# Masked attention on one core: a second, transposed score matmul in place of normalised and turned probabilities

## The reference, cut to what matters

```python
src_trans = (einsum('bsf,of->bso', src, W_src) + b_src) * src_mask[:, :, None]
tgt_trans = (einsum('btf,of->bto', tgt, W_tgt) + b_tgt) * tgt_mask[:, :, None]
src_key, src_val = jnp.split(src_trans, 2, axis=2)
scores = einsum('bthd,bshd->bhts', q, k) / np.sqrt(HEAD_DIM)
scores = where(src_mask[:, None, None, :] == 0, -inf, scores)
attn = softmax(scores, axis=-1)
tgt_update = einsum('bhts,bshd->bthd', attn, v).reshape(b, t, OUT_SIZE)
x = x + tanh(g) * (concatenate([tgt, tgt_update], axis=2) @ W_out.T + b_out)
```

## Time and profile before

| what | us |
| --- | --- |
| median of 3 runs | 712.64 (712.11 to 713.82) |
| the profiled execution | 712.77 |
| its span, first to last instruction | 710.7 |
| scores of batch 0 start | 276.31 |
| scores of batch 15 start | 594.39 |

### The profile page before, as it was taken

One profiled execution on the slowest core, in us unless ns is written; L12 is line 12 of the kernel. 1 busy time (PEld: TensorE's weight loads), 2 busy tenths in 40 slices (PEclk: granted clock), 3 DMA queues, 4 the chain that ended last, 5 costly groups with the idle time before them and its releaser, 6 DMA issues.

```text
span 710.7 us, 12199 instructions
## 1 busy us (share of the span) xinstructions
PE 681.4 (96%) x3877; PEld 478.4 (67%) x3877; DVE 512.4 (72%) x976; ACT 418.1 (59%) x1128; POOL 209.7 (30%) x285
## 2 busy tenths in 40 slices
PE   5799899999999999999999999999999998999997
PEld 3565555554544358788888888888888886756654
DVE  7864757776775458898889888888888888734422
ACT  7656665535555535656756657657667657645453
POOL 6564424200110033233343432332323330052110
PEclk9999999999999999999999999999999999999999
DMA  8721108401000004444323444333444323001012
GB/s 260 237 101 60 59 31 253 79 6 56 1 0 1 0 1 119 120 120 119 76 79 88 119 120 100 87 76 94 119 119 92 85 47 74 3 0 60 30 60 89
DMA packets 44970, 57.54 MB, mean 81 GB/s; under 512 B 13018, under 2 KB 23420, under 8 KB 44796
## 3 DMA queue, kind: packets, MB, share of 16 engines
q1 hardware_dynamic: 44924, 56.96, 29.8%
HBM read 27.46 MB, written 4.19 MB: 45 GB/s over the span
## 4 chain that ended last, share of the span: by engine, by line
PE 79%; ACT 7%; DVE 6%; issue 3%; POOL 2%; SPq 1%; DMA 1%; DVEq 0%; ACTq 0%; POOLq 0%
PE bank L1160 11%; PE bank L1456 8%; PE bank L1374 7%; PE bank L1435 7%; PE bank L1172 5%; PE bank L1392 5%; ACT c_p L956 5%; PE bank L1413 4%; PE bank L1449 4%; PE bank L1592 4%; PE bank L1136 3%; PE bank L1582 2%; PE bank L1140 2%; PE bank L1583 2%; DVE c_nmx L1914 2%
## 5 line engine op out<-in xcount | busy, mean ns | idle before, releaser
L956 ACT ACTIVATE c_p<-bank,c_nmx 128x256 f32<-128x256 f32 x256 | 117.3, 487 | 26.2 <-DVE c_nmx L1914 26.2
L1160 PE MATMUL bank<-b_o,cw 128*128 128x512 f32 x192 | 90.8, 603 | 0.2 <-ACT b_o L808 0.2
L1927 DVE TENSOR_TENSOR c_p<-c_p,c_inv 128x1024 f32<-128x1024 f32 x64 | 90.1, 1408 | 1.1
L1914 DVE TENSOR_REDUCE c_nmx<-bank 128x4 f32<-128x1024 f32 x64 | 75.4, 1218 | 13.4 <-PE bank L1413 13.4
L1435 PE MATMUL bank<-ident,c_p 128*128 128x128 f32 x512 | 65.4, 276 | 2.2 <-ACT c_p L956 1.6
L1435 PEld LDWEIGHTS bank<-ident,c_p 128*128 128x128 f32 x512 | 58.2, 142 | 10.0 <-issue 4.5
L784 ACT ACTIVATE b_h<-bank,cb 128x512 f32<-128x512 f32 x48 | 32.8, 686 | 51.2 <-PE bank L1160 51.2
L1059 ACT ACTIVATE d_h<-bank,b_col 128x512 f32<-128x512 f32 x64 | 39.6, 686 | 39.6 <-PE bank L1583 39.6
L1374 PE MATMUL bank<-c_ctxT,wsrcT 128*128 128x256 f32 x256 | 61.4, 385 | 0.7 <-ACT c_ctxT L932 0.7
L1160 PEld LDWEIGHTS bank<-b_o,cw 128*128 128x128 f32 x192 | 34.1, 190 | 41.3 <-issue 39.2
L1934 DVE COPY c_pT<-bank 128x512 f32<-128x512 f32 x64 | 43.7, 685 | 18.0 <-PE bank L1435 18.0
(11 more groups left out here) (194 smaller groups left out, 1384.4 us busy)
## 6 DMA issues: line engine op xcount, KB each, us to landing
c_stack<-c_parts SPq DMA_DIRECT2D x192, 128.0 KB
a_ctx<-in_ctx SPq DMA_DIRECT2D x16, 512.0 KB, 3.8
c_ctx<-in_ctx SPq DMA_DIRECT2D x16, 512.0 KB, 3.5
out_x<-x_sb SPq DMA_DIRECT2D x7, 512.0 KB, 2.9
x_sb<-in_x SPq DMA_DIRECT2D x3, 1024.0 KB, 10.2
mask_b<-in_mask_BxS_fk SPq DMA_DIRECT2D x1, 2048.0 KB, 12.1
x_sb<-in_x SPq DMA_DIRECT2D x2, 512.0 KB, 5.9
wsrc_raw<-in_L_xattn_W_src SPq DMA_DIRECT2D x1, 1024.0 KB, 6.8
```

Source lines behind the costliest of these rows:

```text
L956: op = nc.scalar.activation(c_p[hg][:, tc, j, :], scores(tc)[:, j, :], ACT.Exp, bias=c_nmx[hg][:, tc, j:j + 1], accum_out=c_sum[hg][:, tc, ...
L1160: op = mm(bank[2 * u + h][:], cw1[:, c, h * P:(h + 1) * P], b_o[n % LANES][:, c, :], start=c == 0, stop=c == DK - 1)
L1914: v.tensor_reduce(c_nmx[hg][:, tc, :], scores(tc), AXIS.X, ALU.max, negate=True)\
L1927: v.tensor_tensor(pr, pr, c_inv[hg][:, :, js].unsqueeze(3).to_broadcast([P, TS, 2, S]), ALU.mult)\
```

## The change: what it does

The probabilities are no longer kept, normalised and turned. The exps of the scores are taken only for their sums, into a bf16 buffer that nobody reads (`c_junk`). From maximum and sum each token and head gets the shift -max - ln(sum), with a correction from 1/sum x sum. It is split into two fp32r parts, turned by PE (4 heads x 2 parts = 8 columns, one transpose per tile), copied by ACT into `c_rows` and moved by a DMA into rows 97 and 98 of the query side of the stack; the key side has ones there. Then the scores are computed a second time with keys as the stationary side, over 99 rows, which gives the transposed and shifted scores in the same banks 0 to 3, and one exp per tile of 1024 elements writes `c_pT` directly. The functions Exp, Ln and Copy are taken from one table set, which is asked for once before the stage.

The weights of keys and queries are loaded with the order of heads and head elements exchanged, so that a stack DMA takes all 128 partitions of a part: 6 DMAs instead of 12, keys and queries apart. `ones_c` fills rows 96 to 98 of both sides. In the last batch, two hidden matmul groups of the next stage are put ahead of the last update. Waits on the old semaphores are replaced by waits on `c_sum_ok`, `c_pT_ok` and others; `scores_free`, `turned_bank` and `ASIDE` are gone. Cut to its core:

```diff
 # SP
-            def stack_c(b, s): ... 12 DMAs, then neg_row
+            def sides_c(b, s, side, firsts):
+                for c, part in enumerate(firsts):
+                    sp.dma_start(c_stack[s][c * HD:(c + 1) * HD, side, ...], c_parts[:, part, ...]).then_inc(c_stack_in, 16)
+            def keys_c(b, s):
+                need(sp, c_k_split, 2 * b + 2)
+                need(sp, c_sT_ps, 2 * TS * (b - 1))
+                sides_c(b, s, 1, (K_HI, K_HI, K_LO))
+            def queries_c(b, s):
+                need(sp, c_qlo_ok, b + 1)
+                sides_c(b, s, 0, (Q_HI, Q_LO, Q_HI))
+                ... neg_row DMA
+            def rows_c(b, s, hg):
+                sp.wait_ge(c_rows_ok, 2 * b + hg + 1)
+                sp.dma_start(c_stack[s][MASK_ROW + 1:MASK_ROW + 1 + SHIFTS, 0, :, hg, :], c_rows[hg][:]).then_inc(c_rows_in, 16)
+            for b in range(B):   # after keys, queries of 0 and stream 2
+                rows_c(b - 1, ., 1); keys_c(b + 1, .); rows_c(b, ., 0); queries_c(b + 1, .); stream_c(b + 3, .)
+            rows_c(B - 1, 1, 1)
 # ACT
-            def exps_c(b, hg, tc):        # into c_p
-            def probsT_c(b, hg, heads):   # copies bank -> c_pT
+            def sums_c(b, hg, tc):
+                need(act, c_mx_ok, TS * n + tc + 1)
+                need(act, c_shift_ok, n - 1)
+                for j in range(QH):
+                    op = nc.scalar.activation(c_junk[:, tc, j, :], scores(tc)[:, j, :], ACT.Exp,
+                                              bias=c_nmx[hg][:, tc, j:j + 1], accum_out=c_sum[hg][:, tc, j:j + 1])
+                op.then_inc(c_sum_ok, 1)
+            def logs_c(b, hg):
+                need(act, c_sum_ok, TS * (n + 1))
+                nc.scalar.activation(c_ln[hg][:], c_sum[hg][:], ACT.Ln).then_inc(c_ln_ok, 1)
+                need(act, c_ln_ok, n + 1)
+                nc.scalar.activation(c_inv[hg][:], c_ln[hg][:], ACT.Exp, scale=-1.0).then_inc(c_inv_ok, 1)
+            def rows_c(b, hg):
+                need(act, c_rows_ps, n + 1)
+                nc.scalar.copy(c_rows[hg][:], bank[6][0:SHIFTS * QH, hg * S:(hg + 1) * S]).then_inc(c_rows_ok, 1)
+            def probsT_c(b, hg, q):
+                need(act, c_sT_ps, TS * n + q + 1)
+                nc.scalar.activation(c_pT[hg][:, :, q * S:(q + 1) * S], scores(q), ACT.Exp).then_inc(c_pT_ok, 1)
 # order on ACT in body_c
+                rows(b-1,1), sums(b,0,0), sums(b,0,1), logs(b,0), probsT(b-1,1,0), high_q, probsT(b-1,1,1),
+                ctxT, update(b-1,1), v, ctxT, rows(b,0), sums(b,1,0), sums(b,1,1), logs(b,1),
+                probsT(b,0,0), probsT(b,0,1), xnT, xnTq, update(b,0)
+            nc.scalar.preload_act_table_set("natural_log_exp_and_others")
 # PE
+            def rows_c(b, hg):
+                need(pe, c_shift_ok, n + 1)
+                need(pe, c_up_ok, n - 1 if is_last(b, B) and hg == 1 else n)
+                for tc in range(TS):
+                    op = nc.tensor.transpose(bank[6][0:SHIFTS * QH, hg * S + tc * P:hg * S + (tc + 1) * P],
+                                             c_shift[hg][:, tc, :, :] as [128, 8], ident[:])
+                op.then_inc(c_rows_ps, 1)
+            def scoresT_c(b, s, hg, q):
+                need(pe, c_rows_in, 16 * (n + 1))
+                need(pe, c_sum_ok, TS * (n + 1) + q + 1)      # the last half: c_pT_ok
+                for j in range(QH):
+                    op = mm(scores(q)[:, j, :], c_stack[s][rows, 1, j, hg, q * P:(q + 1) * P],
+                            c_stack[s][rows, 0, j, hg, :], start=True, stop=True)
+                op.then_inc(c_sT_ps, 1)
 # order on PE in body_c
+                scores(b,0), rows(b-1,1), q, v0, scoresT(b-1,1,0), ctxT, scoresT(b-1,1,1), out_begin(b-1), v1,
+                update(b-1,1), scores(b,1), ctxT, rows(b,0), out(b-1), k first half, scoresT(b,0,0), scoresT(b,0,1),
+                k second half, xnT, update(b,0)
 # order on PE in last_c and after it
+                scores(b,0), rows(b-1,1), lowrank_d(0), xnT_d(1,1), out_begin(b-1), scoresT(b-1,1,0), scoresT(b-1,1,1),
+                scores(b,1), update(b-1,1), xnT_d(1,0), rows(b,0), out(b-1), scoresT(b,0,0), lowrank_d(1),
+                scoresT(b,0,1), rows(b,1), update(b,0)
+            out_begin(b), scoresT(b,1,0), scoresT(b,1,1), hidden_d(0,0), hidden_d(0,1), update(b,1), out(b)
 # DVE
-            inverse_c, normalise_c, probsT_c
+            def shift_c(b, hg):   # five operations on [128, TS, QH], each waits for the one before
+                c_fix = c_inv * c_sum;  c_fix = c_fix - 1 + c_ln;  c_fix = c_nmx - c_fix
+                c_shift hi = c_fix (to fp32r);  c_shift lo = c_fix - hi
+            # in body_c: shift(b,0) before v(b+1) and maxima(b,1); shift(b,1) after finish(b-1)
 # POOL
-                nc.gpsimd.memset(c_stack[s][MASK_ROW:MASK_ROW + 1, 0, :, :, :], 1.0)
+                nc.gpsimd.memset(c_stack[s][MASK_ROW:MASK_ROW + 1 + SHIFTS, :, :, :, :], 1.0)
```

More of the change, by code:

```diff
@@ L64 @@
 MASK_ROW = 3 * HD
-STACK_DMAS = 3 * QH + 1
+STACK_DMAS = 7
+SHIFTS = 2
 LEAD = 2
@@ L516, in stream_c @@
                 sp.dma_start(c_ctx[s][:], ctx_dram[b]).then_inc(c_ctx_in[s], 16)
-            def stack_c(b, s):
-                if isinstance(b, int) and b == 1:
-                    sp.wait_ge(b_ok[3], 2 * PAIRS)
[L521 to L529, removed]
+            def sides_c(b, s, side, firsts):
+                for c, part in enumerate(firsts):
+                    sp.dma_start(
+                        c_stack[s][c * HD:(c + 1) * HD, side, :, :, :].rearrange("p j g t -> p j (g t)").bitcast(F32),
+                        c_parts[:, part, :, :].rearrange("p g t -> p (g t)").bitcast(F32)).then_inc(c_stack_in, 16)
+            def keys_c(b, s):
+                if b == 1:
+                    sp.wait_ge(b_ok[3], 2 * PAIRS)
+                need(sp, c_k_split, 2 * b + 2)
[4 more added lines that the diff above has]
+                sides_c(b, s, 0, (Q_HI, Q_LO, Q_HI))
+                if b < 2:
+                    sp.wait_ge(s_ones, b + 1)
                 sp.dma_start(
@@ L1004, in body_c @@
                     return
-                exps_c(b, 0, 0)
-                exps_c(b, 0, 1)
                 if not first:
-                    probsT_c(b - 1, 1)
-                if not last:
-                    high_q(b + 1)
+                    rows_c(b - 1, 1)
+                sums_c(b, 0, 0)
+                sums_c(b, 0, 1)
+                logs_c(b, 0)
+                if not first:
+                    probsT_c(b - 1, 1, 0)
+                high_q(b + 1)
+                if not first:
+                    probsT_c(b - 1, 1, 1)
                 if ahead:
@@ L1415, in scores_c @@
                     op.then_inc(c_s_ps, 1)
-            def probsT_c(b, hg, heads=range(QH)):
+            def rows_c(b, hg):
                 n = 2 * b + hg
[L1419 to L1431, removed]
-                            pe.wait_ge((c_pT_act, c_pT_dve)[j % 2], QH // 2 * n + 1)
-                    for q in range(TS):
-                        for tc in range(TS):
-                            op = nc.tensor.transpose(
-                                bank[turned_bank(n, j)][:, q * S + tc * P:q * S + (tc + 1) * P],
-                                c_p[hg][:, tc, j, q * P:(q + 1) * P], ident[:])
-                    op.then_inc(c_pT_ps, 1)
@@ L1516, in body_c @@
                 scores_c(b, s, 0)
-                if not last:
-                    q_c(b + 1, 1 - s)
-                    v_c(b + 1, 1 - s, 0)
+                if not first:
+                    rows_c(b - 1, 1)
+                q_c(b + 1, 1 - s)
+                v_c(b + 1, 1 - s, 0)
                 if first:
@@ L1526, in body_c @@
                 if not first:
-                    probsT_c(b - 1, 1, range(2, QH))
-                if not first:
+                    scoresT_c(b - 1, 1 - s, 1, 1)
                     out_begin(b - 1, 1 - s)
-                if not last:
-                    v_c(b + 1, 1 - s, 1)
+                v_c(b + 1, 1 - s, 1)
                 if not first:
```

253 lines of the change are left out of this document (133 added, 120 removed).

## The result

The changed kernel takes **738.25 us** (median of 4 runs, 734.92 to 742.33) against 712.61 (712.11 to 713.82): a ratio of 1.036, 95% interval 1.0306 to 1.0414. It is slower by 25.6 us. The forecast was 703.8 with a range of 698.5 to 712, and 0.15 for slower. The profiled execution took 737.84 us (span 735.4, mean clock 0.985; before 712.77 and 710.7).

A forecast was written before the change was run, and what follows sets the result against it. PE, busy for 96% of the span, was taken as the bound. Thirteen middle batches -10.4, first batch -1.2, batch 14 -0.3 and the end +2.9 sum to -9.0: 712.8 became 703.8 us, range 698.5 to 712.

The forecast's parts named there:

- the paragraph on SP: SP's stack DMAs: six issue in 3.8 us where twelve took 7.68; the rows' new trip takes 2.4 us.
- the batch by hand: Hand timeline of one middle batch: queries' DMAs landed by 18.5 us, next scores at 20.66, saving 0.8 us per batch.
- late rows: Rival: the rows' DMA queues behind stack DMAs on SP, 4.5 us instead of 2.4, giving 733 us; 12%.
- The floor: PE's work per middle batch: 20.21 us, with 0.45 of waits a period of 20.66; rival without those waits 10%.
- The stall before the second transposed tile: PE in each batch's first half waits for the exps' sums before the second transposed scores: 0.35 us lost.
- the four small transposes: PE's new transposes of 8 columns per batch, priced as full ones: 0.44 us.
- ACT and DVE: Per batch: ACT busy about 17 of 20.5 us, large exp 1.02; DVE loses normalisation and copies, gains ten small operations.
- The start: POOL's longer memset of the ones before the first scores: bounded by 0 and 2 us, taken as 0.
- Batch 0: First attention batch: 16 transposes of 2.41 us replaced by matmuls and row transposes of 1.26, so -1.2 us.
- DVE's chain of small operations: Five dependent 8-element operations on DVE per half, 2 us long, covered by PE's 5 us and costed at nothing.
- Batch 14: Last but one batch: 19.6 us against 19.9, so -0.3 us.
- the tail: Last batch's first scores to the first second_d matmul: 28.95 us against 26.05, so +2.9 us.

The follow-up runs named there:

- e1: The changed kernel with the old order of heads and the old twelve stack DMAs of 128 KB, five ahead of the first half's rows: 709.24 us, 0.996 of before.
- e3: The changed kernel, but from batch 2 on the last of three stack pieces on each side copies 16 of 512 elements: 714.88 us, 1.0042 of before.

## Why the prediction was wrong, point by point

**The step that failed** is the paragraph on SP and the line of the batch by hand, "The queries' DMAs go out at 13.5 to 16, landed by 18.5". They went out at 13.6 to 16.2 after the batch's first scores (452.50 and 455.12, less 438.94), and landed at 22.0 (460.94). The rate behind it, "768 KB need 3.1 us" in the rival "late rows", took the mean rate of the old copies at full use (97 GB/s at 39%, so 249). I moved that rate to another pattern of partitions because packets and bytes were the same. At the measured 131 GB/s 768 KB need 6.0 us. The cover was 20.66 - 18.5 = 2.2; landing 3.5 late, it left 1.3 to 1.7 us of wait in most batches. The diff showed the new pattern in plain sight (one DMA reads all of `c_parts`, and the loads were rearranged for it), and it deserved a rival.

**The rival "late rows"** had the right sign and the wrong place. Its sentence on transfers, "both should be gone", was the false one; but the rows' own trip stayed short. Issued at 451.80, they let the transposed scores start at 455.08 without a wait; only in batch 14 did they take about 4 us (issued 605.57, released 609.55); there they were issued 5.3 us behind the first of the keys' DMAs, in the middle 6.0, and 768 KB need about 6. The stack that they queue among was what came late. The sentence that no row shows a small DMA behind a large one was a misreading: the mask row is one, behind twelve of 128 KB. By the Trainium skill, "DMA: Bandwidth & Descriptors", Queues, rings and completion order, an engine works through one ring in order; the 4 us in batch 14 agree with it, the middle batches show no sign of it.

**The floor was right.** With the old DMAs the period is 20.49 undisturbed and 20.64 on average over batches 1 to 13 (e1), forecast 20.66. Inside, two terms were off: eight transposed score matmuls take 455.08 to 456.23, 0.144 each and not 0.13, and the update waits for nothing where 0.1 was taken. The stall before the second transposed tile is 0.23 (forecast 0.35), the four small transposes 0.45 (0.44).

**ACT and DVE were right.** The changed kernel's groups:

```profile
L1001 ACT ACTIVATE c_pT<-bank 128x1024 f32<-128x1024 f32 x64 | 63.4, 1020 | 3.6 <-PE bank L1488 2.5
...
L989 ACT ACTIVATE c_inv<-c_ln 128x8 f32<-128x8 f32 x32 | 6.7, 209 | 1.0
```

The large exp takes 1.02 us (forecast 1.02; the two copies behind that sum differ by 0.87 ns per element, not 0.84, which would give 1.04), Ln and Exp of 8 elements 0.21 (0.19), the row copy 0.36 (at most 0.375). There are four table loads, as before: Ln and Exp need no switch. The Trainium skill, "ScalarE: Activation LUTs", Table sets, has both in one set, and this trace agrees.

**The start** was mis-sized at 0 out of a bound of 0 to 2. The memset took 3.52 us on the chain where 1.81 stood: +1.7, which e1 keeps (first scores at 278.01). The slow copies added the rest of the 6.3, as the changed kernel's chain shows. Behind the wait of 6.11 the granted clock was 0.57:

```profile
261.85 3.52 POOL c_stack L711
...
271.43 10.94 DMA c_stack<-neg_row
282.37 0.25 issue
282.62 2.04 PE bank L1463 x8
284.66 3.02 PE bank L1449 x8
```

```profile
282.00:288.00 6.00, 5.38 (x19) 4.77 (x20) 2.63 (x3) 2.89 (x13) 5.37 (x3) 0.57 0.56 125
```

Eight scores take 2.04 instead of 1.18 us and the queries 3.02 instead of 1.73: part of this stretch ran at the 1.2 GHz level. That is 2.15 of batch 0's 2.8, and the same happened at 614.90 in the last batch, behind a wait of 1.51 (2.08 for the scores). The prediction has no clock term, neither here nor in its last batch, where it has PE wait.

**Batch 0** was forecast at -1.2 and came to 19.68 in e1, +0.34. I cost DVE's chain of small operations "at nothing"; here it had no cover. Of the five, e1's DVE shows:

```profile
285.08 1.13 DVE L1990 SCALAR_TENSOR_TENSOR c_fix<-c_fix,c_ln 128x8 f32<-128x8 f32 x1
286.25 1.19 DVE L1993 TENSOR_TENSOR c_fix<-c_nmx,c_fix 128x8 f32<-128x8 f32 x1
```

```profile
284.91 1.28 POOL L713 TENSOR_TENSOR c_parts<-c_qT,c_parts 128x512 fp32r<-128x512 f32 x1 [1.42 <-ACT c_parts L968]
...
286.15 1.27 POOL L700 TENSOR_TENSOR x_sb<-x_sb,bout_b 128x512 f32<-128x512 f32 x1
```

Their median is 0.17; these two lasted until POOL's operation of 128x512 beside them ended (286.2, 287.4).

**Batch 14 and the tail.** Batch 14 takes 21.68 in e1, of which 2.14 is the wait for the stack of batch 15; without it 19.54, forecast 19.6. The last batch takes 29.03 in e1, forecast 28.95, but that match is in part luck. In e3 no wait stands ahead of batch 15: its batch 14 takes 19.45, and its last batch 30.36. The two together were forecast at 48.55 and take 49.81 in e3 and 50.71 in e1, so of the 2.2 that e1 lost there 0.9 goes with the wait, and by e3 1.3 would stay. What stays includes clock. In the last batch PE waits for exps and is then slow, here in e3:

```profile
597.00:600.00 3.00, 1.20 (x8) 0.85 (x8) 1.14 (x6) 2.94 (x10) 0.00 (x0) 1.00 0.00 0
600.00:603.00 3.00, 2.88 (x20) 1.86 (x23) 2.30 (x2) 1.08 (x2) 0.00 (x0) 0.61 0.00 0
```

The second scores and the update took 2.05 and 1.94 us there, where e1 shows 1.55 and 1.07.

So with the old DMAs the sum would have been: start +1.7, batch 0 +0.3, thirteen batches -10.5, batch 14 +1.8, tail +3.0, together -3.7. The forecast of -9.0 missed 5.3 even there: 1.7 by the memset, 1.5 in batch 0 and 2.2 in the last two batches, all at the ends.

## What to carry to other kernels

When a change rewrites a DMA's access pattern, price its rate anew, even if bytes and packets stay the same: compare GB/s at full DMA use, with the partitions read and the partitions written as part of the form. A transfer that is hidden "by 2 us" is the first thing to lose when its rate falls by a third; and a wait on PE can cost clock on top: here waits of 6.11 and of 1.51 us were followed by first scores at the 1.2 GHz level, other waits of 1.3 to 1.7 us were not. Before more cover is built around a slow transfer, try the old form of it beside the new computation: here one run gave back 29 us.

## What the hardware did that I had not expected

- **Copies within SBUF depend on what they read.** 2 KB packets, 16 engines: reading 32 neighbouring partitions, 200 GB/s at 87% use, with neighbouring or strided writes alike; reading every fourth partition into 32 neighbours, 155 GB/s at 96% in the usual batch; reading 128 or 64 neighbours folded four to one, 127 to 132 GB/s at 97% use and more. The Trainium skill, "SBUF — State Buffer", The DMA setup-cost knee, advises 128 partitions and the largest single transfer; the six larger DMAs over 128 partitions followed it on the reading side, and here the measurement goes the other way. What in the hardware does it was not settled: no run separated the number of partitions read from which ones they are, or the fold from either.
- **Small DVE operations stretch beside POOL.** 0.17 us became 1.13 and 1.19, as above, in two of 160 in e1. The same page, Who interferes with whom, says that a DVE operation with two SBUF inputs contends with one of GpSimd that reads SBUF; this trace agrees for these two. It isn't every operation of POOL: 22 operations of the same chain with two SBUF inputs ran wholly beside its TENSOR_TENSOR of 128x2 into `rstd` (0.73 us) and took 0.17 to 0.20. The TENSOR_SCALAR that took 3.20 in place of 0.73 has only one tensor input; whether it fell under that page's rule for two-port modes no row shows.
